# Three seams of a two-layer tower: preparing steps begun in the first attention, the softmax attention's first item inside their last two, the last output chain among the experts

## The reference

```python
h = take(W.T, x) + b + positions                      # (2, 2048, 128)
# first block, 8 heads of 16, no softmax
q, k, v = split(layernorm(h) @ w_qkv)
dots = where(causal, q @ k.T * scale, 0)
t = dots - mean_so_far(dots);  s = mean_so_far(t * t)
attn = where(causal, t * rsqrt(s + 1e-8) * norm_g + norm_b, 0)
h = h + (attn @ v) @ w_out + b_out
# second block: normalised twice, 2 heads of 64, softmax, then 8 experts
hx = layernorm_affine(layernorm(h))
q, k = l2norm(hx @ Wq) * 8 * qn_g, l2norm(hx @ Wk) * 8 * kn_g
o = softmax(where(causal, q @ k.T / 8, min)) @ (hx @ Wv)
y = o @ Wo;  gate = softmax(y @ gate_W + gate_b)
h = h + sum_e gate_e * (gelu(y @ W1_e + b1_e) @ W2_e + b2_e)
```

## Time and profile before

| | us |
|---|---|
| median of 3 runs (957.13 to 965.5) | 964.89 |
| the profiled execution | 964.4 |
| its span, first to last instruction | 962.3 |
| PE busy | 827.2 (86%) |
| DVE busy | 732.0 (76%) |
| ACT busy | 513.4 (53%) |
| POOL busy | 366.6 (38%) |

### The profile page before, as it was taken

How to read it: one execution, slowest core, us unless ns; L and a number is a source line. 1 busy time by engine, 2 the same in 40 slices (tenths; PEclk the granted TensorE clock), 3 DMA queues, 4 the chain that set the end, 5 groups by cost and what they waited for, 6 DMA issues and landing times.

```text
span 962.3 us, 21449 instructions
## 1 busy us (share of the span) xinstructions
PE 827.2 (86%) x7864; PEld 592.4 (62%) x7864; DVE 732.0 (76%) x1725; ACT 513.4 (53%) x1069; POOL 366.6 (38%) x478
## 2 busy tenths in 40 slices
PE   1677999999667565888898998699999999999997
PEld 1555777777433333556665666477777777777775
DVE  5736666666579896667667774399999999999997
ACT  1322444444056765667686898455555555555553
POOL 7565555555567774455565676100000000000000
PEclk9887999999656766899999999799999999999999
DMA  3110000000001110000000000000000000000000
GB/s 124 46 26 4 1 0 0 0 0 0 1 22 43 33 41 16 1 1 2 2 2 1 2 2 2 1 2 13 2 12 2 13 3 11 13 2 13 2 13 12
DMA packets 9474, 11.65 MB, mean 12 GB/s; under 512 B 1832, under 2 KB 6704, under 8 KB 9264
## 3 DMA queue, kind: packets, MB, share of 16 engines
q1 hardware_dynamic: 8368, 8.43, 2.9%
q0 software_dynamic: 1024, 2.10, 0.8%
...
## 4 chain that ended last, share of the span: by engine, by line
PE 60%; DVE 11%; POOL 11%; issue 9%; ACT 7%; DMA 0%; DVEq 0%; POOLq 0%; ACTq 0%
PE ps L897 59%; POOL plo L359 3%; DVE mx L794 2%; DVE y L684 2%; ACT phi L520 2%; POOL h_all L221 2%; ACT p L519 1%; POOL rr L306 1%; POOL rr L315 1%; DVE x L726 1%; DVE ss L732 1%; POOL ss L323 1%; ACT ql L506 1%; ACT arena L408 1%; PE ps L1167 0%
## 5 line engine op out<-in xcount | busy, mean ns | idle before, releaser
L897 PE MATMUL ps<-y,arena 128*128 128x512 f16 (+1 forms) x896 | 247.4, 424 | 19.3 <-DVE y L684 17.0
L548 ACT ACTIVATE cst<-ps,col 128x512 f32<-128x512 f32 x256 | 176.1, 688 | 163.6 <-PE ps L897 163.6
L897 PEld LDWEIGHTS ps<-arena,sq 128*128 128x128 f16 x3072 | 192.8, 98 | 60.5 <-DVE sq L883 0.7
L897 PE MATMUL ps<-arena,sq 128*128 128x128 f16 x3072 | 213.0, 219 | 0.5 <-DVE sq L883 0.5
L883 DVE TENSOR_TENSOR sq<-cst,sq 128x512 f16<-128x512 f32 x256 | 175.7, 686 | 4.4
L359 POOL TENSOR_TENSOR plo<-p,phi 128x512 f16<-128x512 f32 (+2 forms) x120 | 124.8, 1058 | 89.8 <-ACT phi L520 88.2
L878 DVE CAST sq<-cst 128x512 f16<-128x512 f32 x256 | 108.0, 422 | 12.2 <-ACT cst L548 3.1
L897 PEld LDWEIGHTS ps<-y,arena 128*128 128x128 f16 (+1 forms) x896 | 75.4, 112 | 58.5 <-issue 24.8
L794 DVE TENSOR_REDUCE mx<-ps 128x1 f32<-128x512 f32 (+3 forms) x160 | 91.3, 604 | 24.6 <-PE ps L897 23.8
L519 ACT ACTIVATE p<-ps 128x512 f32<-128x512 f32 (+3 forms) x160 | 88.2, 552 | 23.8 <-PE ps L897 22.6
L520 ACT ACTIVATE phi<-ps 128x512 f16<-128x512 f32 (+3 forms) x160 | 88.7, 554 | 0.0
...
## 6 DMA issues: line engine op xcount, KB each, us to landing
...
h_all<-emb_rows,idx POOLq DMA_INDIRECT x32
...
```

The lines of the kernel that those rows point to most:

```text
L548: a.activation(hid[:, f], ps[:, HBANK[f], :], ACT.Gelu_apprx_tanh, bias=col[:, K_B1 + k:K_B1 + k + 1], scale=1.0 / WS).then_inc(S["hid_rea ...
L897: return t_.matmul(o, l, r, start=start, stop=stop, skip_group_check=True)
```

## The change

**Preparing begun earlier.** The last two chunks of the first attention are taken out of their loops and written together with the start of preparing: `stats2` and `normed2` of chunks 0 and 1, their transposes and projections lie under chunk 15. The last chunk no longer forms a state. Its variances, outputs and `h1_out` lie in preparing steps 0, 1 and 3. Both normalisations come from one formula, so that DVE makes one small operation (`two_norms`) and POOL one power. In a step the projection is now of c + 2 and stands behind `unit_T`, and the low halves of chunk c - 1 are made in step c.

**First item inside the last two steps.** Row maxima of item 0 are formed in steps 8 to 12. After step 13 the first scores follow; steps 14 and 15 stand behind scores 0 and 2. Item 1's maxima use bank 2 alone, item 0's bank 7. The split of the weights leaves the preparing stage: its 16 pieces stand behind steps 6, 14, ..., 126 of the softmax attention.

**Last output chain among the experts.** The experts' slices use bank 7 in place of 4, and the five parts of the last chain stand behind `down` slices 1, 6, 11, 18 and 23.

```diff
-        rr = [sb(f"rr{i}", [P, 4, B]) for i in range(2)]
-        x2 = [sb(f"x2{i}", [P, B, D]) for i in range(2)]
-        hxT = [sb(f"hxT{i}", [P, B, P]) for i in range(2)]
+        rr = [sb(f"rr{i}", [P, 2, B]) for i in range(2)]
+        x2_all = sb("x2", [P, 2, B, D])
+        hxT_all = sb("hxT", [P, 2, B, P])
+        x2 = [x2_all[:, i] for i in range(2)]
+        hxT = [hxT_all[:, i] for i in range(2)]
...
-        MB = [2, 3, 5]
         RING = 4
-        HBANK = [0, 1, 4, 5]
+        HBANK = [0, 1, 5, 7]
+        LAST = B * NQ - 1
...
+            for n in range(2, NPIECE):
+                sp.wait_ge(S["wlow_ready"], n - 1)
+                sp.dma_start(stage[n % 2], w12_rows[:, n * 512:(n + 1) * 512]).then_inc(S[STAGED[n % 2]], 16)
...
+            def both_norms(c):
+                par = c % 2
                 pool.wait_ge(S["stats2"], c + 1)
...
+                g.tensor_tensor(rr[par][:, 1], rr[par][:, 0], mhalf[:, 0:B], ALU.pow).then_inc(S["rr_ready"], 1)
+
...
+            coefs(NT - 3)
+            state_add(NT - 2)
+            both_norms(0)
+            out_bias(NT - 1)
+            both_norms(1)
+            coefs(NT - 2)
+            both_norms(2)
+            l2_factors(0)
+            for c in range(NT):
+                if c + 1 < NT:
+                    l2_factors(c + 1)
+                if c + 3 < NT:
+                    both_norms(c + 3)
+                if c == 0:
+                    coefs(NT - 1)
+
+            def weights_low(n):
+                piece = w12[:, 4 * n:4 * n + 4]
+                pool.wait_ge(S["whigh_ready"], n + 1)
+                g.tensor_tensor(piece[:, :, 1, :], scaled[n % 2].rearrange("p (w d) -> p w d", d=D),
+                                piece[:, :, 0, :], ALU.subtract).then_inc(S["wlow_ready"], 1)
+
...
+                if k in WSLOT:
+                    weights_low(WSLOT.index(k))
...
+            normed_T(0)
+            squares(0)
+            for b in range(B):
+                sums_out(NT - 1, 1, b)
+            normed_T(1)
+            ao_out(NT - 2)
+
+            def step_b(c):
+                if c + 1 < NT:
+                    squares(c + 1)
+                if c == 2:
+                    ao_out(NT - 1)
+                if c + 2 < NT:
+                    normed_T(c + 2)
                 high_qk(c)
...
+                    if k == 0:
+                        high_qk(NT - 2)
+                    if k == 2:
+                        high_qk(NT - 1)
...
+                    if k in WSLOT:
+                        weights_high(WSLOT.index(k))
+                for m in range(LAST):
+                    out_part(m, (k - YAT[m]) / YGAP)
...
+                    if n * FT + f in ACT_AT:
+                        out_part(LAST, ACT_AT.index(n * FT + f) + 1)
...
+            def two_norms(c):
+                par = c % 2
+                dve.wait_ge(S["agg2"], c + 1)
+                v.tensor_scalar(rr[par][:, 0], mv2[par][:, :, 1], 1.0 + LN_EPS, LN_EPS * LN_EPS, ALU.mult, ALU.add
+                                ).then_inc(S["stats2"], 1)
...
+            variances(NT - 3, 1)
+            masked(NT - 2, 0)
+            state_out(NT - 2, 0)
+            dve.wait_ge(S["h1_ready"], NT - 3)
+            stats2(0)
+            two_norms(0)
+            masked(NT - 2, 1)
+            state_out(NT - 2, 1)
+            outputs(NT - 3, 1)
+            stats2(1)
+            two_norms(1)
+            h1_out(NT - 3)
+            variances(NT - 2, 0)
+            masked(NT - 1, 0)
+            normed2(0)
+            masked(NT - 1, 1)
+            outputs(NT - 2, 0)
+            normed2(1)
+            stats2(2)
+            two_norms(2)
+            h1_out(NT - 2)
+            sum_squares(0)
+            low_v(0)
+
+            def step_b(c):
+                unit_qk(c)
+                if c + 2 < NT:
+                    normed2(c + 2)
+                if c:
+                    low_qk(c - 1, 0)
+                if c + 1 < NT:
+                    sum_squares(c + 1)
+                if c:
+                    low_qk(c - 1, 1)
+                if c == 3:
+                    h1_out(NT - 1)
+                if c + 3 < NT:
+                    if c + 3 >= NT - 2:
+                        dve.wait_ge(S["h1_ready"], c + 4)
+                    stats2(c + 3)
+                    two_norms(c + 3)
+                if c + 1 < NT:
+                    low_v(c + 1)
+                if c == 0:
+                    variances(NT - 1, 1)
+                if c == 1:
+                    outputs(NT - 1, 1)
...
+            for c in range(BTAIL):
+                step_b(c)
+                if 9 <= c < 13:
+                    row_max(0, MPARTS[0][c - 9])
+            unit_qk(NT - 2)
+            low_qk(NT - 3, 0)
+            sum_squares(NT - 1)
+            low_qk(NT - 3, 1)
+            low_v(NT - 1)
...
+                if k == 1:
+                    unit_qk(NT - 1)
+                    for b in range(B):
+                        low_qk(NT - 2, b)
+                if k == 4:
+                    for b in range(B):
+                        low_qk(NT - 1, b)
...
+            c, cur = NT - 1, 1
+            for b in range(B):
+                pe.wait_ge(S["qkT_sb"], c + 1)
+                pe.wait_ge(S["dt_sb"], 2 * c + b)
+                dots(cur, b, kT, qv)
+                sums(c, cur, b, state=False)
+                if b == 0:
+                    normed_T(0)
+            project2(0)
+            for b in range(B):
+                pe.wait_ge(S["dt_sb"], 2 * c + b + 1)
+                for h in range(HA):
+                    at = D + h * XW
+                    last = mm(ps[:, 5 + b, at:at + XW], dtm[:, b, h], kv[cur][:, b, h], start=False)
+                last.then_inc(S["x_ps"], 1)
+            normed_T(1)
+            out_T(NT - 2)
+            out_project(NT - 2)
+            project2(1)
+
+            def step_b(c):
+                if c + 2 < NT:
+                    normed_T(c + 2)
                 unit_T(c)
+                if c + 2 < NT:
+                    project2(c + 2)
+                if c == 1:
+                    pe.wait_ge(S["hxT_sb"], 4)
+                    out_T(NT - 1)
+                if c == 2:
+                    pe.wait_ge(S["hxT_sb"], 5)
+                    out_project(NT - 1)
...
+                if k == 0:
+                    step_b(NT - 2)
+                if k == 2:
+                    step_b(NT - 1)
...
+                    if n * FT + f in PE_AT:
+                        out_part(LAST, PE_AT.index(n * FT + f) + 1)
...
+BTAIL = NT - 2
 PR, QR = 5, 4
 LAG = 3
 YGAP = 3
 ITEMS, STEPS, FIRST, MPARTS, MSLOT, OAT, YAT = plan()
 NSTEP = len(STEPS)
+NMAX = sum(len(p) for p in MPARTS)
+PE_AT, ACT_AT, DVE_AT = [1, 6, 11, 18, 23], [5, 10, 16, 22], [12, 16, 24]
+WSLOT = [8 * n + 6 for n in range(2 * E * FF // 512)]
+
+
+def max_bank(k):
+    return 7 if k < 4 else 2 if k < 8 else (2, 3, 5)[k % 3]
+
+
+def row_bank(it):
+    return 7 if it == 0 else 5 if it == 1 else 4
+
+
+def x2_bank(c):
+    return 1 if c == 0 else 3 if c == 1 else 0
 
 
 def on_pool(k):
```

509 lines of the change are left out of this document (226 added, 283 removed).

## The result

The changed kernel takes 934.7 us (median of 4 runs, 931.2 to 936.4) against 961.35 for the kernel before (4 runs, 957.1 to 965.5). The ratio is 0.970, with a 95% interval of 0.967 to 0.974: 27 us saved, where 25.0 were forecast. Its profiled execution took 936.1 us with a span of 934.3; the forecast was 939.4 and 937.3. The outcome is the forecast, not a rival.

The account below looks back on a forecast made before the run. PE bounds the experts, DVE with its waits the preparing loop; in the softmax attention PE and ACT are close to full. -12.5 - 20.7 + 9 + 8 - 8.8 = -25.0 us: span 937.3, time 939.4, range 918 to 955.

Parts of the forecast that it names:

- A: First seam, first attention to preparing: first unit_qk at 257.4 instead of 269.9, gain 12.5 us, bounds 10 and 14.
- first unit_qk near 257: Sign for the first seam in the new profile: preparing's first unit_qk starts near 257 us.
- B: Preparing loop: step from 6.98 to 6.0 us without POOL's chain and the collision, fourteen steps before the scores, gain 20.7.
- Rival 3: Preparing step does not get shorter, held at 6.9 us by the PE and ACT loop: 952 us, chance 0.08.
- C: Two preparing steps inside the softmax attention's first item: cost 9 us, from added unit_T work and order.
- D: Sixteen weight pieces inside the softmax attention, 1.04 us each on ACT: cost 8 us, bounds 0 and 17.
- E: Last seam, into the experts: first down 14.1 us earlier, less 4.3 for PE and 1.0 for table loads, gain 8.8.
- 1 (923): Hidden after all: cheaper preparing steps and first item, weight pieces and table loads absorbed: about 923 us, chance 0.20.
- 2 (951): ACT becomes the bound of the softmax attention, weight pieces at 16.6 and first item at 12: 951 us, chance 0.18.
- 4: PE's clock falls in the softmax attention because ACT pieces open gaps on PE, +40 to +45: 980 us, chance 0.06.
- ACT over 36 of 40 us: Sign for the weight pieces: ACT busier than 36 of 40 us in the softmax attention up to the 126th step.

Follow-up runs that it names:

- e7: Changed kernel with the Exp of the last gate, inside the experts, made a plain copy, so without its two table loads: 932.6 us, ratio 0.969.
- e14: Changed kernel with PE's transposes of chunk 0 at the first seam placed behind the second batch row's dots and sums of chunk 15: 931.25 us, ratio 0.970.
- e2: Changed kernel with the last output chain ahead of the experts again, the other two seams as changed: 944.05 us, ratio 0.983.
- e3: Changed kernel with preparing steps 14 and 15 ahead of the first scores again: 934.1 us, ratio 0.972.
- e12: Changed kernel with e8's order, e14's later transposes and e1's pieces (now in preparing steps 3 to 12) together: 928.75 us, ratio 0.963.
- e4: Changed kernel with POOL's old chain of seven dependent operations for the norm factor, no weight pieces in the preparing steps: 947.3 us, ratio 0.986.
- e1: Changed kernel with ten of sixteen weight pieces back in preparing steps 4 to 13, the other six in the softmax attention: 932.9 us, ratio 0.971.
- e8: Changed kernel with another order in the first item: unit_qk(15) before item 1's row maxima, chunk 14's low halves behind them, chunk 15's transposes later: 931.5 us, ratio 0.969.
- e11: e4 with both of DVE's low halves behind the square sums: 945.7 us, ratio 0.982.
- e13: e11 with the statistics of chunk c+3 ahead of the low halves too, DVE's order of the kernel before: 944.9 us, ratio 0.984.
- e6: Changed kernel with ACT copying each weight piece a third time, into a buffer nobody reads: 938.0 us, ratio 0.976.

## Why the prediction was right, point by point

**A, first seam.** Forecast -12.5, measured -10.65 from mask to unit. The chain behind PE's block came as priced: 261.87 - 256.16 = 5.7 us from the end of the block (252.01 + 4.15), where 257.4 - 251.8 = 5.6 were forecast. What fell short is the block. It was priced at full clock. After a wait of 1.6 us that the forecast didn't have, PE was granted 0.63 while the projection ran, so mostly its 1.2 GHz level, and 0.85 over the block: 2.31 for the projection that the earlier trace rows shows at 1.53, and 4.15 for 3.66. The window of the projection:

```profile
249.87:252.18 2.31, 2.31 (x8) 1.36 (x6) 1.93 (x9) 0.00 (x0) 0.20 (x1) 0.63 0.00 0
```

e7 has the same wait and then 1.00. The traces at the higher clock give 14.3 - 27.7 = -13.4. So the term is a pair of values, -10.65 and -13.4, around the forecast, and the unforeseen wait itself costs nothing (e14). The other 2.6 us are at the start of the program, in code that the change doesn't touch. The same four products in the kernel before (timeline of PE):

```profile
26.46 1.13 PE L897 MATMUL ps<-y,arena 64*128 64x512 f32 x4
```

and in the changed kernel:

```profile
27.06 2.08 PE L929 MATMUL ps<-y,arena 64*128 64x512 f32 x4
```

At 2.4 GHz they take 1.13, at 1.2 GHz 2.08 us. e2, e3 and e12 have the first, the others 1.92 to 2.08. Absolute times such as my "first unit_qk near 257" (it was 261.9) can't be held to less than this.

**B, preparing loop.** Forecast -20.7, measured -23.2. From the first `unit_qk` to the fifteenth it takes 346.15 - 261.87 = 84.3 us, where 84.0 + 3.4 + 2.0 = 89.4 were forecast: the plain step is 5.79 (6.0 forecast, 5.7 for DVE alone), the first is 4.87, since it has no low halves of a chunk before it, and the added work took 4.1 of its 5.4. From there to the scores it takes 4.3 us instead of 1.7. That tail left out a term, the projection of chunk 15, which PE has in front of the product that makes the row of maxima:

```profile
346.17 2.77 PE L929 MATMUL ps<-wsm,hxT 128*128 128x384 f32 x4
348.73 0.63 PE L929 MATMUL ps<-c,mpad 128*65 128x128 f16 x4
```

The price of the step was right, the reasons for it only half. I had 0.52 us for POOL's chain and 1.0 for the collision of its weight subtraction with DVE's, as if they were two separate terms. The mistake was to read a wait of 0.52 us as the chain's price: taking the pieces away and leaving the chain gains nothing, in the new order at least (e4, 7.03). In the kernel before the step was a ring of POOL and DVE, here one round (POOL, then DVE, then POOL again):

```profile
281.09 0.20 POOL L321 TENSOR_TENSOR ss<-ss,eps 128x8 f32<-128x8 f32 x1 [1.01 <-DVE ss L732]
...
285.61 0.19 POOL L317 TENSOR_TENSOR rr<-rr 128x2 f32<-128x2 f32 x1
285.98 1.33 DVE L726 TENSOR_SCALAR x<-h_all,mv,rr 128x128 f32 x2 [0.68 <-POOL rr L317]
287.24 0.67 DVE L732 TENSOR_REDUCE ss<-qk 128x8 f32<-128x512 f32 x1
287.99 0.20 POOL L321 TENSOR_TENSOR ss<-ss,eps 128x8 f32<-128x8 f32 x1 [1.01 <-DVE ss L732]
```

The factors take 1.9 us, the chain 2.8, the subtractions with what lies around them 1.5, the square sums 0.7: 6.9 in all. The collision is a member of the ring too (1.33 for 0.57), and the two belong together: the chain's last operation releases DVE's subtractions, and POOL's piece stands right behind it (285.82), so they meet in thirteen steps on end. The chain shortened by 2.1 us takes the ring under DVE's own sum, what is gained is the distance to that sum, and a piece then meets the subtractions only in some steps, for 0.8 us each (e1). The change removed both, so these runs don't divide the 23.2 us between them.

Rival 3 would have had PE and ACT hold the step at 6.9. e8 has one plain step wholly at 1.2 GHz (granted 0.50) and another at 2.4 GHz (1.00):

```profile
297.91:304.07 6.16, 5.15 (x15) 3.05 (x14) 5.57 (x17) 3.71 (x10) 2.54 (x4) 0.50 0.00 1
310.14:315.93 5.79, 2.99 (x16) 1.69 (x15) 5.57 (x16) 3.81 (x10) 2.54 (x4) 1.00 0.00 0
```

So the low clock does lengthen a step, by 0.37 us, not by 0.9 or more, and the loop had it only in part (0.93 granted from 300 to 315, 0.68 from 332 to 346).

**C, two steps inside the first item.** Forecast +9, measured +9.6, by the wait foreseen (the third row maximum behind `unit_qk(15)` and the low halves; 3.30 on PE). 13.2 us from the first item's scores to the second's, about 15 forecast. But part of the 9.6 isn't the two steps. Without the weight pieces at the seventh and fifteenth score steps it is 2.85 less (e1), which leaves 6.75 for C; with the pieces kept and the two steps taken out it is 33.45 - 28.2 = 5.25 less (e3). So C itself is 5 to 7 us and was priced too high; the rest belongs to D, and the agreement of 9.6 with 9 is luck. And e8 shows that 2.6 of it was order, not work.

**D, weight pieces in the softmax attention.** Forecast +8. Measured +3.2 behind s16, but this number is two: PE's idle time rose by 27.1 - 20.8 = 6.3 us, and its busy time fell by 3.1, while the clock rose from 0.96 to 0.98. That the idle time is the program's and not chance can be seen in nine kernels that have the same program behind s16 (the changed one, e2, e3, e4, e7, e8, e11, e13, e14): 27.0 to 27.1 us idle in all nine, with busy times from 174.3 to 177.3. With the 2.85 above, the sixteen pieces cost about 9 us, 0.6 each of their 1.04 on ACT; e1, with eight fewer pieces in the stretch, has 4.7 less of it, 0.6 each again. That is near the half that I took. That 3.1 came back in busy time is luck and can't be counted on, as e1 and e12 show with equal programs there. PE's waits for phi went from 3.6 to 7.5 us as foreseen, but ACT was busy 34.6 us of the 40 from 540 to 580, not over the 36 that I named.

**E, last seam.** Forecast -14.1 and +5.3; measured -14.4 and +4.8, and e2 gives the same 9.5 when the seam is undone. Inside the +4.8 two terms failed. The output chain's pieces on PE are 0.44 + 0.91 + 0.86 + 0.44 + 1.2 = 3.85, read from how much longer their `down` slots are than the 1.32 of the others (4.3 forecast). The two table loads are 0, not 1.0 (e7). And 0.9 is lost in the slots where DVE's eight operations of the chain lie, 2.0 us of DVE in all, which I had said would fit under PE's pieces; DVE is 95.95 of 100 us busy in the experts, so it has little room for them, though no run moves them to show it. The two errors of one microsecond cancelled, which is luck. The loads' rows show 1.28 us each, with the Exp starting 0.01 us after the first. The Trainium skill (ScalarE: Activation LUTs, What ACT_TABLE_LOAD costs) counts about 1.4 us of drain on each switch; nothing of it appears in these rows, and e7 shows that the pair as a whole cost nothing.

**The rivals.** 1 (923) didn't come: C and D were not absorbed, with 5 to 7 and about 9 us. 2 (951) didn't come either: ACT doesn't set the pace everywhere, about 0.6 of each piece's 1.04 us is paid; with a third copy it comes nearer, 5.1 of 7.3 us (e6). 3 is answered under B. 4 didn't come: the idle time of PE in the stretch rose by 6.3 us and the granted clock was 0.98. The Trainium skill (TensorE: Matmul & The Clock Gate, A second HAM failure mode) reports that short waits make the clock swing. In this stage the sum of the waits doesn't tell the level: e6, with 32.1 us of idle PE, has 0.98, and e1, with 22.35, has 0.95.

**The sum.** Against the forecast A is 1.85 us dearer, the start of the program 2.6, C 0.6; B is 2.5 cheaper, D 4.8 and E 0.8. Together that is 3.0 us, -28.0 of span for -25.0. So the total is nearer than D alone, and of D's 4.8 the 3.1 of busy time were not earned. Of the signs named ahead, ACT over 36 of 40 us and the first `unit_qk` near 257 were missed.
